# One fused attention kernel, its step loops put in another order on all five engines

## The reference, cut to what matters

```python
def _mha(x, kv, Wq, Wk, Wv, mask, causal):
    Q = einsum('bsd,hdk->bhsk', x, Wq) * m ; K, V likewise from kv
    energy = einsum('bhsk,bhtk->bhst', Q, K)
    lengths = sum(energy[:, :, 0, :] != 0, axis=-1)      # from the first query row
    energy = where(cols >= lengths, -inf, energy)
    if causal: energy = where(cols > rows, -inf, energy)
    score = softmax(energy / sqrt(dk)) ; out = einsum(score, V) * m
...
x1 = layernorm(x + mha(x, x, causal))                     # layer "self"
x2 = layernorm(x1 + mha(x1, ctx))                         # layer "cross"
x3 = layernorm(x2 + fc2(relu(fc1(x2))))
y  = layernorm(x3 + (mha(x3, ctx, with biases) @ Wo + bo))  # layer "outer"
```

## Time and profile before

| | us |
|---|---|
| median of 3 runs | 459.49 |
| the profiled execution, its own time | 457.92 |
| its span, first to last instruction | 456.2 |
| PE busy / weight loads | 384.5 / 280.3 |
| DVE busy | 354.0 |
| ACT busy | 249.2 |
| POOL busy | 111.1 |
| 16 DMA engines, mean share busy | about 24% |

### The profile page before, as it was taken

One profiled execution on the slowest core, in us unless ns is written; L12 is line 12 of the kernel. 1 busy time (PEld: TensorE's weight loads), 2 busy tenths in 40 slices (PEclk: granted clock), 3 DMA queues, 4 the chain that ended last, 5 costly groups with the idle time before them and its releaser, 6 DMA issues.

```text
span 456.2 us, 10986 instructions
## 1 busy us (share of the span) xinstructions
PE 384.5 (84%) x3512; PEld 280.3 (61%) x3528; DVE 354.0 (78%) x1144; ACT 249.2 (55%) x557; POOL 111.1 (24%) x261
## 2 busy tenths in 40 slices
PE   0477899887898998989989899898998999889863
PEld 0454655665666666757757677676666667667632
DVE  7456888886898887887977888888787788777753
ACT  3024455544665655655665575665665765656632
POOL 8900012111221120321312132221322122322122
PEclk9989999999999999999999999999999999999987
DMA  5022323203322122222222222222122132232310
GB/s 161 0 53 57 81 62 97 60 19 64 86 59 55 39 61 53 46 62 51 45 64 51 47 53 60 46 56 62 42 58 58 40 77 49 52 65 45 67 26 17
DMA packets 22270, 25.62 MB, mean 56 GB/s; under 512 B 3781, under 2 KB 12742, under 8 KB 22214
## 3 DMA queue, kind: packets, MB, share of 16 engines
q1 hardware_dynamic: 22214, 24.93, 24.2%
HBM read 3.61 MB, written 1.05 MB: 10 GB/s over the span
## 4 chain that ended last, share of the span: by engine, by line
PE 43%; DVE 24%; issue 12%; DMA 8%; ACT 7%; SPq 4%; DVEq 0%; POOL 0%; POOLq 0%; ACTq 0%
DVE negmax L653 10%; PE k_bank L367 7%; DMA spread<-negmax_T 7%; PE score L400 6%; PE attend L425 6%; PE o_bank L442 5%; PE o_bank L452 4%; PE q_bank L367 4%; ACT o_sb L539 3%; PE score L403 2%; ACT high_q L585 2%; DVE x L739 2%; ACT high_k L577 2%; SPq L1064 2%; DVE scaled L734 2%
## 5 line engine op out<-in xcount | busy, mean ns | idle before, releaser
L531 ACT ACTIVATE probs<-attend 128x512 f32<-128x512 f32 x192 | 112.0, 599 | 46.5 <-PE attend L425 23.8
L653 DVE TENSOR_REDUCE negmax<-score 128x4 f32<-128x512 f32 x192 | 126.8, 683 | 13.1 <-PE score L403 7.2
L425 PE MATMUL attend<-spread,packed 128*128 128x512 f32 x192 | 91.1, 479 | 18.5 <-DMA spread<-negmax_T 17.3
L400 PE MATMUL score<-spread,packed 128*128 128x512 f32 x192 | 85.9, 484 | 8.0 <-DVE negmax L653 4.5
L577 ACT ACTIVATE high_k<-k_bank,flags 128x512 fp32r<-128x512 f32 x48 | 33.0, 687 | 76.5 <-PE k_bank L367 76.5
L425 PEld LDWEIGHTS attend<-spread,packed 128*128 128x128 f32 x192 | 36.5, 191 | 33.5 <-DMA spread<-negmax_T 23.2
L400 PEld LDWEIGHTS score<-spread,packed 128*128 128x128 f32 x192 | 36.1, 192 | 30.6 <-DVE negmax L653 25.5
L367 PE MATMUL k_bank<-xc_T,w_packed 128*128 128x128 f32 x384 | 52.4, 281 | 1.8 <-ACT xc_T L558 0.5
L367 PE MATMUL q_bank<-xc_T,w_packed 128*128 128x128 f32 x384 | 52.3, 281 | 0.0
L442 PE MATMUL o_bank<-probs,v_aug 128*32 128x128 f32 x1536 | 52.1, 276 | 0.0
L367 PEld LDWEIGHTS k_bank<-xc_T,w_packed 128*128 128x128 f32 x384 | 49.1, 196 | 2.1 <-ACT xc_T L558 0.8
(11 more groups left out here) (120 smaller groups left out, 629.1 us busy)
## 6 DMA issues: line engine op xcount, KB each, us to landing
spread<-packed SPq DMA_DIRECT2D x192, 96.0 KB
out_dram<-y_out SPq DMA_DIRECT2D x16, 64.0 KB, 1.8
spread<-negmax_T SPq DMA_DIRECT2D x48, 16.0 KB
rows_sb<-rows_dram SPq DMA_DIRECT2D x1, 704.0 KB
w_sb<-weights_dram SPq DMA_DIRECT2D x1, 576.0 KB, 4.2
spread<-len_mask SPq DMA_DIRECT2D x32, 8.0 KB
packed<-len_mask SPq DMA_DIRECT2D x32, 8.0 KB
x_in<-x_dram SPq DMA_DIRECT2D x1, 512.0 KB, 3.6
```

Of the source, the lines that this page charges most:

```text
L400: last = nc.tensor.matmul(dst[:, :], packed[:, s, 0, q, :], spread[:, s, 1, :, q, :], start=True, stop=l != SELF)
L425: last = nc.tensor.matmul(dst[:, :], packed[:, s, 1, q, :], spread[:, s, 0, :, q, :], start=True, stop=l != SELF)
L531: nc.scalar.activation(probs[:, q, :], attend_bank[q % 2][:, :], ACT.Exp, scale=float(DK) ** -0.5).then_inc(exp_done.sem, 1)
L653: nc.vector.tensor_reduce(negmax[:, :].rearrange("p (j q) -> p j q", q=QUADS)[:, :, q], score_bank[q % 2][:, :].rearrange("p (j t) -> p j ...
```

## The change

The bodies of all helper functions stay. Only the five `step` functions change: the order of the calls, and for some the unit that a step works on (a call may move from the end of one step to the start of the next).

- PE: the step begins with the first two scores. `attend` 0 and 1 of the next unit stand at the end, behind the projections and the front transposition of u+4. V is projected between K and Q. `values` stands ahead of `first_scores`, all three tail parts stand earlier, and the two transpositions stand directly ahead of the projections.
- ACT: `mask_ctx` stands ahead of `high_k_parts`, `evacuate_v` between the high parts; `tail_evac(.., 0)` stands between exponentials 1 and 2.
- DVE: `attention_out` 4 and 5 and `tail_out` 4 stand ahead of the two splits, with `attention_out` 6 between them, and the four maxima follow with only `prepare(.., CROSS, 0)` between. `tail_out` 5, the length, and `tail_out` 1 and 2 stand behind the maxima.
- POOL: `spread_first` and `cross_inputs` go to the end of the step before.
- SP: `put_negmax` goes ahead of both `put_length`.

```diff
@@ PE
             def step(u):
-                project(u + 2, 1)
-                project(u + 2, 0)
-                project_v(u + 2)
-                attend(u, 0)
                 score(u + 1, 0)
                 score(u + 1, 1)
-                attend(u, 1)
-                front_transpose(u + 3)
                 attend(u, 2)
+                tail(u - 1, 0)
+                attend(u, 3)
                 score(u + 1, 2)
-                attend(u, 3)
+                tail(u - 1, 1)
                 score(u + 1, 3)
-                tail(u - 1, 0)
+                values(u)
                 first_scores(u + 2)
-                values(u)
+                tail(u - 1, 2)
                 transpose_negmax(u + 1)
-                tail(u - 1, 1)
                 transpose_o(u)
-                tail(u - 1, 2)
+                project(u + 3, 1)
+                project_v(u + 3)
+                project(u + 3, 0)
+                front_transpose(u + 4)
+                attend(u + 1, 0)
+                attend(u + 1, 1)
@@ ACT
             def step(u):
-                exponentials(u, 0)
-                exponentials(u, 1)
-                exponentials(u, 2)
                 exponentials(u, 3)
                 evacuate_x_T(u + 3)
-                tail_evac(u - 1, 0)
+                tail_evac(u - 1, 1)
                 evacuate_o(u)
-                tail_evac(u - 1, 1)
                 evacuate_negmax(u + 1)
+                mask_ctx(u + 4)
                 high_k_parts(u + 3)
+                evacuate_v(u + 3)
                 high_q_parts(u + 3)
-                evacuate_v(u + 3)
-                mask_ctx(u + 4)
+                exponentials(u + 1, 0)
+                exponentials(u + 1, 1)
+                tail_evac(u, 0)
+                exponentials(u + 1, 2)
@@ DVE
             def step(u):
+                attention_out(u - 1, 5)
+                split_k(u + 2)
+                attention_out(u - 1, 6)
+                split_q(u + 2)
                 maxima(u + 1, 0)
-                attention_out(u - 1, 5)
                 maxima(u + 1, 1)
-                attention_out(u - 1, 6)
-                tail_out(u - 2, 5)
+                prepare(u + 4, CROSS, 0)
                 maxima(u + 1, 2)
                 maxima(u + 1, 3)
                 split_maxima(u + 1, 0)
+                split_maxima(u + 1, 1)
+                tail_out(u - 2, 5)
                 length_mask(u + 2, 0)
-                split_maxima(u + 1, 1)
+                tail_out(u - 1, 1)
                 length_mask(u + 2, 1)
+                tail_out(u - 1, 2)
                 length_mask(u + 2, 2)
                 length_mask(u + 2, 3)
                 attention_out(u, 0)
+                tail_out(u - 1, 3)
+                attention_out(u, 1)
+                prepare(u + 4, CROSS, 1)
+                attention_out(u, 2)
                 prepare(u + 2, SELF, 0)
-                tail_out(u - 1, 1)
+                attention_out(u, 3)
                 prepare(u + 2, SELF, 1)
-                prepare(u + 4, CROSS, 0)
-                tail_out(u - 1, 2)
-                prepare(u + 4, CROSS, 1)
-                attention_out(u, 1)
-                tail_out(u - 1, 3)
-                attention_out(u, 2)
-                attention_out(u, 3)
-                split_k(u + 3)
+                attention_out(u, 4)
                 tail_out(u - 1, 4)
-                split_q(u + 3)
-                attention_out(u, 4)
@@ POOL
             def step(u):
-                spread_first(u + 2)
-                cross_inputs(u - 1)
                 outer_inputs(u)
                 tail_rstd(u - 1)
                 attention_rstd(u)
+                spread_first(u + 3)
+                cross_inputs(u)
@@ SP
             def step(u):
                 put_spread(u + 2)
+                put_negmax(u + 1)
                 put_length(u + 2, 0)
-                put_negmax(u + 1)
                 put_length(u + 2, 1)
                 store(u - 2)
```

## The result

The changed kernel takes 444.64 us (median of 4 runs, 442.48 to 447.09) against 459.62 us for the kernel before on the same chips. The profiled execution takes 445.08 us with a span of 443.4 us, so 12.8 us less span than before. The forecast was 437.5 us in a range from 424 to 456: the direction and the range held, but of 22 us forecast the medians show 15.0 and the two profiled spans 12.8.

A forecast was written before the change was run, and what follows sets the result against it. Two loops of nearly one length, DVE waiting for the transposed output and PE for the maxima's transfer, bound the steps. Middle 13.7, early 6 and late 2.7 us, taken as 22, give 437.5 us, range 424 to 456.

The forecast's parts named there:

- Which waits go: DVE's wait before the reciprocal falls from 42 to under 15 us, PE's for the maxima's transfer from 17.3 to under 5.
- SP's swap: On SP the maxima's transfer no longer stands behind the length and could start 1.0 us earlier in a step.
- The middle: The 24 middle steps fall from 8.57 to 8.0 us each, 13.7 us in all.
- the length: Later length transfers delay scores by nothing to 0.3 us a step, taken as 0 because DVE reaches its first maximum later.
- V between K and Q: On PE, Q comes 0.22 us later, a loss in steps where PE sets the pace.
- The tail ahead of attend 3: tail 0 waits for split_q on PE, hidden by DVE, taken as nothing; uncovered, 0.2 to 0.3 us a step.
- mask_ctx: On ACT it delays K's high part by up to 0.6 us; counted 0 in heavy steps, 0.2 on average in others.
- The early stretch: The first 12 steps gain 0.7 us each, less 2.5 for a stall at unit 4's front transposition: 6 us.
- half the gain: Rival, chance 0.18: transfer behind the spread or tail holding attend 3 costs 0.2 to 0.35 us a step; 448.5 us.
- more gain: Rival, chance 0.08: DVE becomes nearly gapless, 7.6 us a middle step, time 424 us.
- nothing: Rival, chance 0.05: PE's latency chain is underestimated by its hand-overs, every step ends at 8.5 us; 458 to 460 us.
- The slower rival: Chance 0.12: dependent attention_out parts ahead of split_k on DVE take 3.1 us, not 2.0; 469 us at 1.0 extra per step.

The follow-up runs named there:

- e2: e1 with SP's first length transfer ahead of the maxima's again, as in the kernel before: 462.86 us, ratio 1.007.
- e5: The kernel before with one edit, SP's maxima transfer ahead of the first length transfer: 459.48 us, ratio 0.9991.
- e9: e8 without the two length transfers and the waits for them, so the output can be wrong: 436.16 us, ratio 0.9493.
- e8: e1 with V projected ahead of the output's transposition, the waits for its inputs in front of it: 441.17 us, ratio 0.9579.
- e7: e1 with V projected behind Q and evacuated behind the high part of Q, as before: 459.78 us, ratio 0.9997.
- e11: e1 with DVE's attention_out 4 to 6 and tail_out 4 around the splits and first maxima as before: 466.12 us, ratio 1.0133.
- e4: e1 with prepare(.., CROSS, 1) directly behind the third maximum on DVE: 442.42 us, ratio 0.9617.
- e1: The changed kernel with the load of x sequences 4 to 7 issued at SP's start instead of in step 0: 441.1 us, ratio 0.9582.
- e12: The kernel before with the load of x sequences 4 to 7 at the start, alone: 460.14 us, ratio 1.0002.
- e6: e1 with the tail's first transposition behind attend 3 on PE and its copy behind exponential 2 on ACT: 449.17 us, ratio 0.9757.

## Why the prediction came out as it did

- *Which waits go.* Right, in kind: DVE's wait for the output and PE's for the maxima's transfer fell as forecast, and e2 shows that there is no gain without the second. What was to come in their place is wrong: PE's waits for `split_q` before the tail's transposition are 0.2 us, and those for maxima before scores fell from 4.5 to 1.8 us. PE waits for ACT's copy of the output instead, 8.9 us. The sum treated SP's swap as one term of 1.0 us; e2 and e5 show it isn't a term but a condition. Alone it is worth nothing, without it the rest is worth less than nothing.
- *The middle.* 24 x (8.57 - 8.10) = 11.3 us against 13.7. The term that was mis-sized is the length: "cost nothing to 0.3 us in a step; I take 0". The argument was that DVE reaches its first maximum later than the score anyway. In the step shown above that fails: the chain is PE's, 0.34 us of waiting stand on it, and DVE waits 0.34 us for that score. e9, against e8, prices the transfers at 2.7 us in the 24 middle steps, which covers the miss of 2.4.
- *V between K and Q.* Entered as a cost of 0.22 us, which it also is; what it buys, that V is out before the front transposition, was left without a price. e7: 18.7 us.
- *The tail ahead of attend 3.* Taken as nothing, and it is hidden as argued as long as x2 is ready before `split_q` ends. e11 shows the price when that cover is gone: not the 0.2 to 0.3 us that the text gave, but 1.3 us and more in each step with a cross tail, since attend, score and maximum queue behind it.
- *mask_ctx.* Right: ACT waits 23.6 us, and e4 shows them covered.
- *The early stretch.* This is the largest miss: 1.6 us gained (12 x (9.17 - 9.03)) where 6 were forecast, 8.4 less 2.5 for a stall. The stall at unit 4's front transposition was named and priced at 2.5 us. PE waited 3.3 us, and then worked at the lower of its two clock levels, granted 0.50 and 0.66 in the two windows after: 12 matmuls of 512 columns started 0.44 us apart and not 0.23, some 2.5 us more. The step is 5.9 us longer than e1's. That second half had no term. Without the stall, in e1, the 12 steps take 102.7 us, a gain of 7.3 where the forecast has 8.4, so some 1.1 us of the miss lie elsewhere.
- *The ends.* The first transposition of the maxima comes 0.86 us later and the end after the last takes 1.1 us more (16.7 against 15.6). Neither was in the sum, and neither is shown to come from the change. e12, whose engines keep the old order, has its first transposition at 36.77, later than the changed kernel's. e5, whose PE, ACT and DVE keep it too, takes 17.5 us after the last, with the clock at 0.50 where the trace of before had 1.00, as the windows of before and then of e5 show:

```profile
444.00:448.00 4.00, 3.26 (x40) 1.80 (x41) 0.35 (x1) 2.92 (x6) 0.76 (x3) 1.00 0.06 16
444.00:448.00 4.00, 3.74 (x37) 2.08 (x35) 0.35 (x1) 2.33 (x5) 0.26 (x1) 0.50 0.06 16
```

- *The late stretch.* 1.8 us for 2.7.

The misses are 2.4 + 4.4 + 2.0 + 0.9 = 9.7 us, which takes 22.4 to 12.7, the 12.8 of the spans but for rounding. The time lies inside the range, and there was luck in where: 444.64 is just under 445, where the forecast's band ends and that of "half the gain" begins, two of the four runs lie above it, and the gain, 15.0 by the medians and 12.8 by the spans, is nearer to the 11 of that rival than to the 22 forecast. Of the rivals, "more gain" and "nothing" are out; "half the gain" gave a time of 448.5 and came near in size, but not for its reasons: attend 0 waits in 4 steps only, and e6 shows the earlier place of the tail and its copy to be a gain. The slower rival, dependent operations ahead of `split_k`, has a price of about 0.3 us a step in e11's first seven, under the 0.7 from which it would decide, and undoing it costs 25 us elsewhere.

The Trainium skill (DMA: Bandwidth & Descriptors, section Queues, rings and completion order) states that a transfer's semaphore increment lands only after every earlier write of the same DMA engine. The price that the prediction feared from this does not show. In one of the four waits of the changed kernel the maxima's transfer was issued 0.04 us after the issue of the last spread transfer had ended:

```profile
102.49 2.44 SPq L1046 DMA_DIRECT2D spread<-packed  x3
104.97 0.67 SPq L1033 DMA_DIRECT2D spread<-negmax_T  x1
107.32 0.50 PE L425 MATMUL attend<-spread,packed 128*128 128x512 f32 x1 [0.47 <-DMA spread<-negmax_T]
```

PE uses it 2.35 us after its issue. In the 21 waits of the kernel before, most of them with 1.7 to 2.9 us between the two issues, the median is 2.39 us.

## What to carry to other kernels

When two waits end a step at nearly the same time, an edit that shortens one is worth nothing alone and may decide everything together with others: try the set, then take single parts out of the set, rather than putting them in one by one. For each call that moves a step earlier, look for the load that it waits for, in the first steps too, where loads are issued from inside the same loop. And when a stall of the matmul engine is priced, add the slower clock that can follow it: 2.5 us behind 3.3 here.

## What was not expected of the hardware

- After PE stood still for 3.3 us in the changed kernel, its clock was at half until about 56.8 us, 5.8 us after it had started again; it was already there before the start (0.50 from 50 to 51 us). In e12 the same followed a wait of 3.17 us for the maxima's transfer in the step of the bias transfers: 0.65 and 0.84 in the windows from 104 to 116 us, and a step of 13.75 us. The kernel before has a wait of 3.17 us for the same transfer at that place, too, and was granted the full clock in its trace, with a step of 11.11 us. In e5, in the same step, a wait of 2.55 us goes with 0.66 and 0.91 from 104 to 112 and a step of 11.85 us. In e11 three waits of 1.6 to 1.7 us for x2 have a low clock behind them (0.51 to 0.68), and three of the same length, before 325.57, 376.93 and 394.16 us, have 1.00. So the low clock can follow such a wait and need not; what decides it isn't shown. The e12 windows:

```profile
104.00:112.00 8.00, 4.83 (x15) 3.01 (x14) 3.41 (x8) 2.52 (x7) 2.03 (x5) 0.65 0.38 80
112.00:116.00 4.00, 3.75 (x48) 2.48 (x47) 2.47 (x9) 2.50 (x7) 0.00 (x0) 0.84 0.02 4
```

- The runs of the changed kernel spread over 1.0% (442.48 to 447.09), those of e1 over 0.13% (440.72 to 441.3), with 4 runs each. That the stall causes the spread does not follow: e9's runs, with the early load, spread over 1.0% too (433.09 to 437.34), and e11's over 0.8%. What differs between traces of the same stretch is the granted clock near the start and the end (0.73 and 0.84 from 30 to 38 us in e1, 0.50 in e8 from 34 to 38, 1.00 in the changed kernel). How much of the spread that is isn't shown.
